# A four-layer graph network on one core: coefficients as columns, halved norm factors, the mean by ScalarE, GpSimd's long operations in pieces, and a new order of steps

## The reference, cut to what matters

```python
h = jnp.maximum(_layernorm(x, axis=-1), 0.0)   # before every layer
x = x + layer(h, adj, ...)

# layer 0: pairwise attention, its coefficients from pairs of consecutive entries of the flattened n x n matrix
h = x @ others_weight;  u1 = h @ a1;  u2 = h @ a2
e = leaky(u1[:, idx1] + u2[:, idx2], 0.1)      # softmax over axis 1, masked by adj
out = einsum('bik,bkl->bil', att, h) + x @ self_weight
# layer 1: attention times A, layernorm, relu; then h_gin = (1 + eps) * h_gat + A @ h_gat; two dense layers with a
# layernorm between them; relu(x_gin + h_gat)
# layer 2: attention, bias, elu;  a row without neighbours gets the mean over all nodes
# layer 3: softmax of listed edge values; diagonal part @ (h W0) + the rest @ (h W1) + bias
```

## Time and profile before

| | before |
|---|---|
| median of 3 runs | 1011.76 us (1009.36 to 1011.84) |
| profiled execution, its own time | 1009.46 us |
| its span, first to last instruction | 1007.7 us |
| TensorE busy | 943.0 us, 7355 matmul instructions |
| VectorE busy | 866.1 us |
| ScalarE busy | 632.5 us |
| GpSimd busy | 566.6 us |
| mean granted clock of TensorE | 0.979 |

### The profile page before, as it was taken

How to read it: one execution, slowest core, us unless ns; L and a number is a source line. 1 busy time by engine, 2 the same in 40 slices (tenths; PEclk the granted TensorE clock), 3 DMA queues, 4 the chain that set the end, 5 groups by cost and what they waited for, 6 DMA issues and landing times. The chain is left out here.

```text
span 1007.7 us, 21096 instructions
## 1 busy us (share of the span) xinstructions
PE 943.0 (94%) x7355; PEld 901.4 (89%) x7355; DVE 866.1 (86%) x2526; ACT 632.5 (63%) x1655; POOL 566.6 (56%) x1171
## 2 busy tenths in 40 slices
PE   5879999999999989999989999999999999997998
PEld 4779998998988989998989999899999998997897
DVE  6879898899979999978989987789989887887973
ACT  3435746875777755676675756777458676666751
POOL 3416356655477662763748645736646475556750
PEclk9978999999999999999999999999999999999999
DMA  5011000000011010011000101100100100000012
GB/s 136 1 36 28 2 1 1 2 1 1 2 43 42 2 44 1 1 43 43 2 1 2 43 2 43 43 1 13 32 1 2 42 2 1 17 7 2 1 43 63
DMA packets 38069, 19.97 MB, mean 20 GB/s; under 512 B 3142, under 2 KB 37452, under 8 KB 37964
## 3 DMA queue, kind: packets, MB, share of 16 engines
q1 hardware_dynamic: 36080, 18.42, 6.6%
q10 hardware_dynamic: 1884, 0.21, 0.2%
HBM read 10.23 MB, written 8.39 MB: 18 GB/s over the span
## 5 line engine op out<-in xcount | busy, mean ns | idle before, releaser
L450 ACT ACTIVATE Y<-X,SM 128x128 f32<-128x128 f32 x512 | 204.3, 489 | 70.8 <-POOL SM L446 70.6
L687 PE MATMUL ps<-HE,PT 128*128 128x129 f32 x2048 | 240.2, 276 | 2.7 <-ACT HE L999 1.7
L687 PEld LDWEIGHTS ps<-HE,PT 128*128 128x128 f32 x2048 | 233.5, 192 | 4.1 <-ACT HE L999 1.9
L1311 DVE SCALAR_TENSOR_TENSOR PT<-ps,CE,maskT 128x512 f32<-128x512 f32 x256 | 173.0, 741 | 13.3 <-PE ps L811 13.0
L442 POOL TENSOR_TENSOR SM<-SM,minus_half 128x8 f32<-128x8 f32 x96 | 162.9, 1696 | 7.6
L431 POOL TENSOR_TENSOR SM<-ST 128x8 f32<-128x8 f32 x96 | 29.7, 310 | 230.8 <-DVE ST L1176 230.8
L687 PE MATMUL ps<-W,HT 128*128 128x128 f32 (+1 forms) x768 | 125.9, 312 | 0.0
L687 PEld LDWEIGHTS ps<-W,HT 128*128 128x128 f32 x768 | 116.4, 194 | 8.8
L1176 DVE BATCH_NORM_STATS2 ST<-X 128x6 f32<-128x128 f32 x512 | 104.7, 277 | 2.6 <-DMA X<-in_x_dram 1.0
L704 PE MATMUL ps<-ident,Y 128*128 128x128 f32 x640 | 86.3, 282 | 13.2 <-ACT Y L450 11.0
L704 PEld LDWEIGHTS ps<-ident,Y 128*128 128x128 f32 x640 | 74.5, 146 | 16.8 <-ACT Y L450 14.1
(11 more groups left out here) (260 smaller groups left out, 2355.5 us busy)
## 6 DMA issues: line engine op xcount, KB each, us to landing
X<-in_x_dram SPq DMA_DIRECT2D x32, 256.0 KB, 3.5
out_dram<-X SPq DMA_DIRECT2D x32, 256.0 KB, 2.8
adj_raw<-in_adj_dram SPq DMA_DIRECT2D x4, 256.0 KB, 3.8
W<-in_L_gnn_W_dram SPq DMA_DIRECT2D x2, 64.0 KB, 3.8
W<-in_L_gnn_W_dram SPq DMA_DIRECT2D x1, 128.0 KB, 3.5
bias<-in_L_gnn_bias_dram SPq DMA_DIRECT2D x2, 64.0 KB, 3.9
Wo<-L_gnn_others_weight_dram ACTq DMA_DIRECT2D x1, 64.0 KB, 3.2
feat1w<-in_L_gnn_Wp_dram ACTq DMA_DIRECT2D x1, 64.0 KB, 3.6
```

The source lines that it names most:

```text
L450: a = nc.scalar.activation(dst[:, n, 0:F], src[:, n, 0:F], func, scale=SM[s][:, S_RSTD, n:n + 1], bias=SM[s][:, S_SHIFT, n:n + 1])
L687: return nc.tensor.matmul(o, w, m, start=start, stop=stop, skip_group_check=True)
L1311: a = V.scalar_tensor_tensor(out=PT[r][:, j, :], in0=o, scalar=CE[s][:, c:c + 1], in1=maskT[:, j, :].bitcast(F32), op0=ALU.max, op1=ALU.mult)
```

## The change

Five things change together.

1. The coefficients of layer 0 come out of `feat0`: its weights get two more columns (`feat0w`, 130 wide), so its tiles, now three, hold `h`, `u1` and `u2`. ScalarE copies them into `HE` and frees the PSUM. A new step `ucol0` (VectorE) takes the two columns, sets them apart for even and odd nodes by a factor of 0 or 1, and splits them into a high and a low part (`UC`). `coef0` (TensorE) is then 2 matmuls of 32 columns with a constant matrix `halve`, which picks every second node. `split0` (VectorE) reads `HE` in SBUF: two operations of 1,024 columns in place of four of 512 from PSUM.
2. `rstd_of` no longer doubles its factor. The 2 goes into ScalarE's transposed copies (`scale=2.0`) and, once, into `gat_g` and `mlp_g`. The norm in layer 1 needs no reciprocal: it adds the square of the row sum times the epsilon.
3. `gin1` computes the same 640 columns of `HI` in 256 + 384 in place of 512 + 128, with a matrix `gin_mix` that holds the low part of the diagonal block beside two blocks of the mask.
4. ScalarE writes the mean of layer 2 at once into `HT` (four operations of 256 columns), and GpSimd's `mean2` loses its product.
5. GpSimd's `low0`, `mean2` and `shift3` are each four operations of 256 columns in place of one of 1,024.

The strings of turns and banks are all new. A set-up part makes `halve`, `parity` and `gin_mix` once.

```diff
-    "pe": ("gggg01011200201g100221313240030410041013314041252513132052025521243143232013031535040003100110104511"
+    "pe": ("gggg010100212g10012021412343030403410010315012452151153305022231231320430422013010053503101101041124"
...
@@ rstd_of
             if inv:
-                link(TT(sm[:, S_VAR, :], sm[:, S_VAR, :], sm[:, S_INV, :], ALU.mult))
-                link(TT(sm[:, S_VAR, :], sm[:, S_VAR, :], sm[:, S_INV, :], ALU.mult))
-                link(TS(sm[:, S_VAR, :], sm[:, S_VAR, :], 4.0 * LN_EPS, None, ALU.add))
+                link(TT(sm[:, S_VAR, :], sm[:, S_VAR, :], sm[:, S_INV, :], ALU.add))
             link(TT(sm[:, S_RSTD, :], sm[:, S_VAR, :], minus_half[:], ALU.pow))
-            if inv:
-                link(TT(sm[:, S_RSTD, :], sm[:, S_RSTD, :], sm[:, S_INV, :], ALU.mult))
-            link(TS(sm[:, S_RSTD, :], sm[:, S_RSTD, :], 2.0, None, ALU.mult))
             return TT(sm[:, S_SHIFT, :], sm[:, S_RSTD, :], sm[:, S_MEAN, :], ALU.mult)
@@ TensorE
                 def coef0(u, s):
-                    for b in range(G):
-                        turned(u, "norm0", s, b)
+                    pe.wait_ge(sig["ucols"][s], count(u.g, 1, 0))
                     o, done = open_tile(u, "coef0", s, 0)
-                    for t in range(HALF):
-                        for odd in range(2):
-                            for b in range(G):
-                                c = 4 * ((t * 2 + odd) * G + b)
-                                r0 = t * 2 * P + odd
-                                mm = MM(o[:, c:c + 4], HT[s][:, b, r0:r0 + 2 * P - 1:2], wcols0[:], True, True)
+                    cols = UC[s][:].rearrange("p t c l -> p t (c l)")
+                    for h in range(2):
+                        mm = MM(o[:, 0:4 * TG].rearrange("p (t c) -> p t c", t=HALF), halve[:, h, :], cols[:, h::2, :],
+                                h == 0, h == 1)
                     mm.then_inc(done, 1)
                 def feat0(u, s):
-                    for h in range(2):
-                        o, done = open_tile(u, "feat0", s, h)
-                        for tt in range(2):
-                            for b in range(G):
-                                c = (tt * G + b) * F
-                                mm = MM(o[:, c:c + F], blk(s, b, 2 * h + tt), Wo[:], True, True)
+                    for b in range(G):
+                        turned(u, "norm0", s, b)
+                    for n in range(3):
+                        o, done = open_tile(u, "feat0", s, n)
+                        for c, r in enumerate(range(3 * n, min(3 * n + 3, TG))):
+                            mm = MM(o[:, c * WD:(c + 1) * WD], blk(s, r % G, r // G), feat0w[:], True, True)
                         mm.then_inc(done, 1)
@@ gin1
-                            for m in (LO, HI):
-                                MM(o, m[s][:, j * G + b, :], gin_hi[:, j, :], j == 0 and m is LO, False)
-                            mm = MM(o[:, j * P:(j + 1) * P], HI[s][:, j * G + b, :], gin_lo[:, j, :], False, j == T - 1)
+                            lo, c = MIX[j]
+                            hi = HI[s][:, j * G + b, :]
+                            MM(o, LO[s][:, j * G + b, :], gin_hi[:, j, :], j == 0, False)
+                            MM(whole(o, j), hi, whole(gin_hi[:, j, :], j), False, False)
+                            first = min(c, j * P)
+                            mm = MM(o[:, first:first + 3 * P], hi, gin_mix[:, j, :], False, j == T - 1)
@@ ScalarE
-                            a = A(HT[s][:, b, :], o, ACT.Relu)
+                            a = A(HT[s][:, b, :], o, ACT.Relu, scale=2.0)
+                def feat0(u, s):
+                    rows = HE[s][:].rearrange("p r c -> p (r c)")
+                    for n in range(3):
+                        o, read = filled(u, "feat0", s, n)
+                        first, last = 3 * n * WD, min(3 * n + 3, TG) * WD
+                        A(rows[:, first:last], o[:, 0:last - first], ACT.Copy).then_inc(read, 1)
                 def sums2(u, s):
-                    A(SR[s][:], o[:, 0:G * P].rearrange("p (b f) -> p b f", b=G), ACT.Copy,
-                      scale=1.0 / N).then_inc(read, 1)
+                    for t in range(T):
+                        a = A(m[:, t, :], o[:, 0:G * F], ACT.Identity, scale=norow[:, t:t + 1])
+                    a.then_inc(read, 1)
@@ GpSimd (low0 and shift3 in the same way)
                 def mean2(u, s):
-                    link(TT(m, repeat(SR[s][:].rearrange("p b f -> p (b f)"), T), bcast(norow[:], G * F), ALU.mult))
-                    TT(m, m, repeat(bias2[:], TG), ALU.add).then_inc(sig["by_pool"][s], 1)
+                    for t in range(T):
+                        r = m[:, t * G:(t + 1) * G, :]
+                        a = TT(r, r, repeat(bias2[:], G), ALU.add)
+                    a.then_inc(sig["by_pool"][s], 1)
@@ VectorE
-                    if sums is not None:
-                        link(V.tensor_scalar(SM[s][:, S_INV, :], sums, TINY, None, ALU.max))
-                        V.reciprocal(SM[s][:, S_INV, :], SM[s][:, S_INV, :])
+                def ucol0(u, s):
+                    for n in range(3):
+                        read_by_act(u, "feat0", s, n)
+                    src = HE[s][:, :, F:F + 2].rearrange("p (t b) c -> p t b c", b=G)
+                    both = US[s][:].rearrange("p t (o b c) -> p t o b c", o=2, b=G)
+                    for odd in range(2):
+                        a = V.tensor_scalar(both[:, :, odd], src, parity[:, odd:odd + 1], None, ALU.mult)
+                    link(a)
+                    link(V.tensor_copy(UC[s][:, :, :, 0], US[s][:]))
+                    V.tensor_tensor(UC[s][:, :, :, 1], US[s][:], UC[s][:, :, :, 0].bitcast(F32),
+                                    ALU.subtract).then_inc(sig["ucols"][s], 1)
                 def split0(u, s):
-                        a = V.tensor_tensor(YF[s][:, r, :], v, bcast(SM[s][:, S_A, r], F), ALU.mult)
-                        V.tensor_tensor(VA[s][:, r, :], v, bcast(SM[s][:, S_B, r], F), ALU.mult).then_inc(read, 1)
+                    V.tensor_tensor(YF[s], VA[s], bcast(SM[s][:, S_A, :], F), ALU.mult).then_inc(sig["scaled"][s], 1)
+                    V.tensor_tensor(VA[s], VA[s], bcast(SM[s][:, S_B, :], F), ALU.mult).then_inc(sig["scaled"][s], 1)
```

More of the change, by code:

```diff
@@ L55 @@
     ("norm0", 2, "pe act"),
+    ("feat0", 3, "pe act"),
+    ("ucol0", 0, "dve"),
     ("coef0", 1, "pe dve"),
     ("cmax0", 1, "pe dve act"),
-    ("feat0", 2, "pe"),
     ("coefp0", 0, "pool"),
@@ L297, in gnn_kernel @@
         x_loaded = [sem(f"x_loaded_{s}") for s in range(NS)]
-        Y, LOW, HE, LOWB, HT, HI, ST, US, CD, CF, CE, CS, MX, SM, DS, HS, SR = ([] for _ in range(17))
+        Y, LOW, HE, LOWB, HT, HI, ST, US, UC, CD, CF, CE, CS, MX, SM, DS, HS = ([] for _ in range(17))
         def slot_first(s):
@@ L628, in _ @@
                 V.tensor_copy(feat2w[:, F + 1:F + 2], wv[:, 4:5])
+                dve.wait_ge(made["evens"], 1)
+                link(V.reduce_sum(parity[:, 0:1], evens[:], AX_X))
+                V.tensor_scalar(parity[:, 1:2], parity[:, 0:1], -1.0, 1.0, ALU.mult, ALU.add)
                 dve.wait_ge(loaded["vectors"], 16 * len(VECTORS))
@@ L836, in attend, with whole @@
                             mm.then_inc(done, 1)
+                def whole(ap, j):
+                    if j in (0, T - 1):
+                        return ap.rearrange("p (k c) -> p k c", c=P)[:, 0::T - 1, :]
+                    return ap[:, (j - 1) * 2 * P:j * 2 * P]
                 def gin1(u, s):
@@ L972, in split0 @@
                 def split0(u, s):
[L974 removed]
+                    act.wait_ge(sig["scaled"][s], count(u.g, 2, 0))
                     A(HI[s][:], YF[s], ACT.Copy).then_inc(sig["hi"][s], 1)
[L976 to L978 removed]
+                    act.wait_ge(sig["scaled"][s], count(u.g, 2, 1))
                     if u.group > 0:
@@ L1477, in _ @@
                     "stat0": stat0, "stat1": stat, "stat2": stat, "stat3": stat, "coef0": coef0, "cmax0": cmax0,
-                    "coefb0": coefb0, "split0": split0, "low0": low0, "agg0": agg0, "self0": self0, "gats1": gats1,
-                    "gat1": gat1, "gatl1": gatl1, "mlps1": mlps1, "mlpc1": mlpc1, "elu2": elu2,
+                    "ucol0": ucol0, "coefb0": coefb0, "split0": split0, "low0": low0, "agg0": agg0, "self0": self0,
+                    "gats1": gats1, "gat1": gat1, "gatl1": gatl1, "mlps1": mlps1, "mlpc1": mlpc1, "elu2": elu2,
                     "feat3": feat3, "agg3": agg3,
```

149 lines of the change are left out of this document (84 added, 65 removed).

## The result

| | before | changed |
|---|---|---|
| median of the comparison | 1011.8 us (1009.36 to 1012.96, 4 runs) | 973.84 us (973.68 to 974.96, 4 runs) |
| profiled execution, and its span | 1009.46, 1007.7 us | 973.94, 972.0 us |
| mean granted clock of it | 0.979 | 0.984 |

The ratio is 0.963, with an interval of 0.9611 to 0.9649: 35.5 to 39.4 us less. The forecast was 975.

A forecast was written before the change was run, and what follows sets the result against it. TensorE was taken to set the time. From a 1007.7 us span, -32 (TensorE), -1 (norm chain) and +1 (start) gave 975.7, profiled 977.5; less idle time, -2 or -3, gave 975. Range of 8 in 10: 962 to 990.

The forecast's parts named there:

- TensorE, coefficients: coef0 on TensorE: 256 recorded fp32 instructions become 32 fp32r matmuls, -27 us, bounds 21 and 29 less.
- TensorE, `gin1`: gin1's 128 blocks on TensorE: each from 0.56 to 0.525 us, -5.5 us in all, bounds 0 and -7.
- TensorE, `feat0`: feat0 on TensorE: 130 columns for 128 on 256 instructions, +0.5 us.
- longest of the small operation: Successor of VectorE's small operation L1297: maximum near 0.9 us, from 2421 ns, with GpSimd's long operations cut in four.
- the start: First groups: longer path from norm0 to coef0, shorter coef0, another order; +1 us, 5 us either way.
- Nearly one for one: What TensorE's queue sheds comes off the span nearly one for one, as long as other engines keep up.
- VectorE's terms: VectorE: divisor -10, split0 -1, ucol0 +11, waiting behind GpSimd -20, new operations exposed to it +3; sum -17 us.
- The one case at 534 us: VectorE's waiting L1173 finished though GpSimd's L1136 started back to back with L1122: VectorE gets in between pieces.
- In the steady state this is slack: Norm chain: each norm ready 0.3 us earlier counts only in the last 107 us, worth -1 us.
- VectorE did not hold TensorE back: Rival: VectorE gets no turn between pieces, its waiting stays and TensorE idles more; 985 to 1000 us, chance 0.15.
- The larger gain: Rival: half of TensorE's idle 29 us goes, as norms and coefficients come earlier; 960 to 966 us, chance 0.15.
- The late coefficients: Rival: ScalarE and ucol0 between feat0 and coef0 delay agg0 by 2.4 us a group; 1015 us, chance 0.04.

The follow-up runs named there:

- the pieces alone: Kernel before, its order and all else unchanged, with GpSimd's long operations in pieces of 256 columns (mean2's product stays whole): 1012.81 us, ratio 1.0028.
- the filling: Changed kernel with 52 matmuls of 512 columns that nobody reads put where TensorE waits in the start: 972.48 us, ratio 0.9629.
- the run with whole operations: Changed kernel with GpSimd's low0, mean2 and shift3 whole again, 1,024 columns each: 985.28 us, ratio 0.9753.
- the operation put back in the norm: Changed kernel with one linked GpSimd operation of 8 columns, multiplying by 1.0, put back in each of 96 norms: 982.13 us, ratio 0.9721.
- banks by rule: Changed kernel and kernel before, each in its own order, every PSUM tile's bank chosen by a simple rule: 1000.89 us and 1043.98 us.
- the old order: Changed kernel's operations in the order of the kernel before, new steps put in where they first have data, banks by the simple rule: 1055.79 us, ratio 1.0463.

## Why the prediction was right, step by step

| term | forecast | measured |
|---|---|---|
| TensorE, coefficients | -27 | -26.8 |
| TensorE, `gin1` | -5.5 | -5.8 |
| a block of `gin1` | 0.525 us | 0.525 us |
| the coefficients' 32 matmuls | under 6 us | 6.2 us |
| TensorE, `feat0` | +0.5 | -2.2 |
| TensorE busy in all | -32, 911 | -36.7, 906.3 |
| VectorE busy | -17, 849 | -18.4, 847.7 |
| longest of the small operation | 0.9 us | 0.776 us |
| ScalarE busy | 674 | 667.4 |
| idle of TensorE from 112 us on | 25 to 30 (steady state) | 26.1 to 876 us, 7.2 after |
| the start | +1 | first `agg0` at 72.05 us for 74.51; 8.6 us more idle from 48 to 112 us, at a higher clock |
| median | 975 | 973.84 |

**What bounds it** held in the main: the span fell by 35.7 us, TensorE's busy time by 36.7, and adding as much work again cost 20.6 to 35.4 us. "Nearly one for one" is too strong for every part: `gin1` undone gave TensorE 5.5 us more and cost 2.1.

**TensorE's terms** were right to half a microsecond where they rest on rows of forms. For `gin1` there is luck in this: 0.56 - 0.525 is 0.035 us a block, 4.5 us, where the forecast wrote 0.04 to 0.05 and took 5.5; the median of before is 0.575, so the 0.05 was right and the 0.56 was short. Its mechanism, the load of `LOW`'s weights behind a longer matmul, fits: with 512 + 128 back (the `gin1` run), the median step of `LOW` is 0.284 us again.

The sum is 4.7 us short. In the trace 43.0 us of the span were at 1.2 GHz before, in pieces at the start and a few short ones later, and 30.7 in the changed kernel; TensorE was busy for 38.2 and 24.5 of them. At half speed 13.7 us less there is nearly 7 us less of busy time. That is why `feat0`, with more columns, got shorter: its median step is 0.112 us in both. The forecast counted the lower clock inside the 33.0 us of the coefficients and nowhere else. This was the missing term; it has both signs (with the pieces alone the clock was lower, with the filling higher), and nothing in the forecast would have given its size.

**VectorE's terms** held, with errors of a few us that cancel. `split0` takes 39.1 us, 2.44 a group for the 2.65 forecast; `ucol0` 12.0, 0.75 for 0.7; the two operations of the divisor had 10.7. What single operations take beyond the median of their form fell from 32.3 to 10.6 us, over all forms. Of this, 4.8 went with L1173 itself; the other 16.9 stand against the forecast's -20 + 3. The working behind that was loose: 8 and 4.8 and as much again are 25.6 us and not 31, and the 4.8 of L1173 stand both in the divisor's 10 us and in the waiting. Of the relief, the pieces by themselves are 13.8 us by the run with whole operations, and 12.5 in the old kernel. The one case at 534 us was no exception: VectorE gets in between two pieces, and the tail is gone.

**What that relief is worth** was mis-sized. The forecast gave the 17 us on VectorE 2 to 3 us of the span, and the shorter norm chain 1. Undone in the finished kernel they cost 11.2 and 8.1. The step that was wrong is the sentence "In the steady state this is slack", with the tenth of VectorE's relief that was to reach TensorE: both losses grow through the steady state, from 1.2 us at 112 to 13.3 at 876 us with whole operations, and from -1.0 to 9.1 with the operation put back in the norm. A row that speaks against it was in the list of waits of the kernel before, TensorE for the normalised rows, and the forecast did not weigh it:

```profile
PE ps L704 <- ACT Y L450: 11.0, 7, 2.3
```

An engine at 98% of a stretch still had a chain behind it that was late in some turns. That the error did not show in the sum is partly luck. One reason is likely, and not tested by itself: such a price is an upper bound, because the order was made for the changed durations, and an edit in it pays for the misfit too. The pieces alone, in an order that was made without them, gave nothing.

**The start** came out about level. The first `agg0`, which waits for the coefficients' path, before and then changed:

```profile
74.51 0.58 PE L687 MATMUL ps<-HI,maskT 128*128 128x256 f32 x1 [4.59 <-DVE LOW L1247]
72.05 0.58 PE L711 MATMUL ps<-HI,maskT 128*128 128x256 f32 x1 [5.92 <-DVE LOW L1296]
```

It starts 2.5 us earlier, and two executions of the changed kernel differ there by 2.2. Up to 112 us TensorE waits longer (17.0 us for 8.4 from 48 us on) and has less of the lower clock. That these two cancel is likely, but no run shows it.

**The rivals.** VectorE did not hold TensorE back to a degree that the sum would show (700 to 800 us: 98.77 of 100, idle time as before), and the long tails on VectorE did not remain. The larger gain did not come: idle time stayed. The late coefficients did not come in this order, and did in the old one. The forecast named that condition by its price alone; that the new order meets it was taken from six groups in flight and from the earlier trace rows, not looked up in the order, and this was the luck in it.

**What stays open**: how the 36 us divide among the parts. In a fitted order the prices overlap (42 to 57 us), and an order fitted to each half of the change was not made. Nor was a new order made for the old operations, so how much of the gain a better order alone would give is untested. Against a large share of it speaks that TensorE's idle time did not fall (64.7 and 65.7 us), and a better order would have to show there first, though the new step may hide such a gain. How the 43 us between the kernels with banks by rule divide between turns and operations is open for the same reason: the old order, as it was tried, does not carry the new operations.

## What to carry to other kernels

Where one engine is at 98% of a long stretch, price a change first by what leaves that engine's queue, form by form; here this gave the time to 0.2%, with some luck. Then look in the list of waits for the chains that this engine still waits for: a chain that is on it costs all along, as the norms did. Undoing one part in a kernel whose order is written out may measure the part and the misfit together, so read it as an upper bound, and hold a control with the same kind of order beside it. If two engines block each other for whole instructions, cut the long ones of the engine that has time: the longest wait is then one piece. Refit the order to it, and measure: in the old order it brought nothing here.

## What the runs showed of the hardware

- **Narrow matmuls and the clock.** The same number of fp32 matmuls, with 34.5 and 36.5 us of own time, cost 35.4 us with 4 columns each and 20.6 with 128; both have a median step of 0.118 us. The granted clock was 0.973 and 0.990. From 48 to 112 us TensorE was busy about the same (53.20 and 52.42 of 64 us) at a clock of 0.78 and 0.84. This is one pair of kernels; the clock also fell without such matmuls, to 0.961 in the old order with its 121.7 us of idle time.
- **A clock that did not pay.** Filling the gaps took the clock of a stretch from 0.79 to 0.93 and the time by 1.6 us, which is within the spread.
- **Eight columns on a long chain.** An operation of 319 ns, 96 times on an engine with 43% of its time free, cost 8.1 us.
- **The step of a matmul depends on the one ahead.** `LOW` with 512 columns took 0.284 us behind 128 columns and 0.233 behind 384.
- **A VectorE operation behind GpSimd.** The longest of 64 small ones took 776, 1326 and 2391 ns with GpSimd operations of 256, 512 and 1,024 columns, for a median of 222 to 223.
